# Running the experts in units of 256 tokens between the edge groups of a graph layer

## The chip, the cores and the metric

The kernel runs on one core of a Trainium2 chip. The metric is the device time of one execution in microseconds (us), as the median of several executions. In the profile PE is TensorE (the matmul engine), PEld its weight loads, DVE is VectorE, ACT is ScalarE, POOL is GpSimd, and SP is SyncE, which here only issues DMAs.

## What is computed

12500 rows of 256 numbers go through a graph layer with 212500 weighted edges and a mixing layer, and then through 8 experts. Each row goes to the one expert with the highest gate value, and each expert takes at most 1954 rows.

```python
xn = layernorm(x)
neighbor = segment_sum(edge_val[:, None] * xn[edge_src], edge_dst)
gnn = leaky(xn @ W1.T + b1 + (neighbor + neighbor * xn) @ W2.T + b2)
x = x + gnn / norm(gnn) + mix(xn)
h = layernorm(x)
idx, prb = argmax and max of softmax(h @ gate_w + gate_b)
hmid = relu(buf @ w1[e] + b1[e])          # buf: the rows of expert e, 1024 hidden
ybuf = hmid @ w2[e] + b2[e]
x = x + nan_to_num(ybuf of the row * prb * kept)
```

## The kernel before

**Stages.** A row tile is 128 rows, so there are 98 tiles. First all rows are normalised and stored to the scratch tensor `xn_d`. Then comes the edge stage, 208 pairs of edge groups. A group is 512 edges sorted by target, whose targets lie in a window of 48 rows. For each pair POOL issues eight indirect gathers of 128 rows of 256 numbers each (L552, in a ring of 24 slots, so three pairs fit); PE multiplies them with selection matrices (`multiply_pair`, L629, 16 matmul records); ACT copies the sums out of PSUM (`copy_pair`, L1348); PE transposes them (`turn_pair`, L638); DVE adds the windows to the accumulator `acc` (`add_group`, L1010), which holds all 12500 rows. A gather of pair p waits for `pair_mm` of pair p-3, that is until PE has used the rows that lie in its slots.

**The order.** It is written out at build time: `side[p]` lists what each engine does beside pair p. Pairs 0 to 55 carry the key and value products (`kv`), pairs 56 to 58 fold the weights, and from pair 59 on "C ticks" finish one row tile after another in nine steps, each step one tick after the last: the matmuls of the mixing and graph layers (L699, L709 to L716), norms on DVE and ACT, the transposes (L724), the gate logits (L734), the stores of the tile to `h2_d` and to `out`. A tile can start when all edge groups that touch it are added, so there is about 0.8 of a tile for each pair until pair 137 and then about 0.48. Routing (argmax, position in the expert's list, a table of rows by expert) runs along with it. What is left after pair 207 is done on its own.

**The experts.** They begin when the table is complete. Their order is by expert, with 4 units of up to 512 rows each, 32 units and 15632 rows in all, since the unused places of each expert are computed as well. SP loads the weights of an expert once (2 MB, L491, L492). POOL splits them into a rounded part and a rest (L565, L568), ACT and DVE split the activations in the same way, and PE computes each product in three passes of a fast 4-byte form (L785, L786, L787). Results are scaled, cleaned of NaN on DVE (L1253 to L1274), and POOL adds them to `out` by indirect DMA (L590), 128 rows at a time. POOL gathers the inputs (L579), 128 rows at a time.

## Time and profile before

| | us |
|---|---|
| median of 3 runs | 3409.26 (3408.21 to 3422.88) |
| profiled execution | 3381.42 |
| its span | 3379.7 |
| edge stage, from its first gather to its last | 106 to 2531 |
| rest of the tiles and of the routing | 2531 to 2613 |
| experts on PE | 2613 to 3359 |
| last of DVE and POOL | 3359 to 3380 |

| engine | busy us | share |
|---|---|---|
| PE | 2372.2 | 70% |
| DVE | 1748.7 | 52% |
| ACT | 1065.7 | 32% |
| POOL | 2087.9 | 62% |

How to read it: shares are means over stages that differ. PE is busy nearly all the time in the expert stage and about two thirds in the edge stage; POOL is the fuller one there. An idle time in the trace names the one that ended it; "issue" means that nothing that the profile shows was waited for, and "remote" that the releaser isn't shown. The granted clock of PE (PEclk) is given for each stretch, 1.00 being 2.4 GHz and 0.50 being 1.2 GHz.

### The profile page before, as it was taken

How to read it: one execution, taken by the hardware profiler on the slowest of the kernel's cores; microseconds unless marked ns; L12 is line 12 of the kernel's file. 1: busy time of each engine (PE TensorE's matmuls, PEld its weight loads, DVE VectorE, ACT ScalarE, POOL GpSimd, SP SyncE). 2: the span in 40 equal slices, each digit the busy share in tenths (PEclk: the TensorE clock that was granted, in tenths of full speed). 3: DMA queues.
4: the chain of work that ended last, by engine and by line, in shares of the span. 5: the costliest groups of instructions: out<-in, count | busy, mean ns of one | idle time of the engine just before them, and what ended most of it. 6: DMA issues, size and time to landing. Idle time of an engine off the chain costs nothing.

```text
span 3379.7 us, 40594 instructions
## 1 busy us (share of the span) xinstructions
PE 2372.2 (70%) x12708; PEld 1702.0 (50%) x12708; DVE 1748.7 (52%) x4466; ACT 1065.7 (32%) x2265; POOL 2087.9 (62%) x1981
## 2 busy tenths in 40 slices
PE   0277777675666757666666766656665999999997
PEld 0033333332344545454544434333344899999997
DVE  7256565553235545454544333333347577777765
ACT  5212211120123333333322212121122555555553
POOL 0466666666666666666666666666662466666663
PEclk9889888987687787787887666676776999999998
DMA  9544444443344444444444434444342221323330
GB/s 293 155 130 135 132 134 133 128 133 107 114 131 138 135 135 134 134 139 132 139 131 124 120 116 121 115 118 120 115 118 92 50 49 50 72 67 68 73 42 7
DMA packets 270446, 386.95 MB, mean 114 GB/s; under 512 B 51560, under 2 KB 210030, under 8 KB 270128
## 3 DMA queue, kind: packets, MB, share of 16 engines
q0 software_dynamic: 105984, 245.21, 27.9%
q1 hardware_dynamic: 123362, 100.70, 9.7%
q10 hardware_dynamic: 40886, 38.41, 3.4%
q8 instruction: 106, 1.74, 0.2%
q14 instruction: 108, 0.88, 0.1%
HBM read 321.97 MB, written 67.21 MB: 115 GB/s over the span
## 4 chain that ended last, share of the span: by engine, by line
PE 34%; another core or an unknown queue 17%; POOL 15%; issue 14%; DVE 12%; ACT 3%; DVEq 2%; DMA 2%; ACTq 0%; SPq 0%; POOLq 0%
POOL rows_sb L552 15%; PE bank L785 7%; PE bank L786 7%; PE bank L787 7%; PE bank L659 4%; PE bank L629 3%; DVEq L1008 2%; DVE arena L1025 1%; DVE s_sb L999 1%; DVE acc L1010 1%; PE bank L795 1%; DVE arena L1090 1%; PE bank L657 1%; PE bank L638 1%
## 5 line engine op out<-in xcount | busy, mean ns | idle before, releaser
L552 POOL DMA_INDIRECT rows_sb<-xn_scratch,src_sb x1664 | 1625.2, 977 | 902.1 <-issue 570.1
L629 PE MATMUL bank<-rows_sb,s_sb 128*48 128x256 f32 x3328 | 588.9, 445 | 263.7 <-issue 201.1
L629 PEld LDWEIGHTS bank<-rows_sb,s_sb 128*48 128x48 f32 x3328 | 248.1, 139 | 544.2 <-issue 414.6
L1010 DVE TENSOR_TENSOR acc<-acc,bank 128x96 f32 x416 | 106.1, 255 | 705.8 <-remote 398.9
L590 POOL DMA_INDIRECT out_dram<-rows_sb,sca_i x128 | 208.1, 1625 | 273.3 <-DVE rows_sb L1274 236.6
L1376 ACT ACT_TABLE_LOAD x95 | 121.9, 1283 | 618.5 <-remote 543.3
L1228 DVE TENSOR_TENSOR hid<-relu,hid 128x512 fp32r<-128x512 f32 (+1 forms) x256 | 198.3, 775 | 215.1 <-ACT relu L1443 198.0
L785 PE MATMUL bank<-w_lo,hid 128*128 128x256 f32 (+1 forms) x1024 | 298.2, 291 | 0.0
L787 PE MATMUL bank<-w_hi,hid 128*128 128x256 f32 (+1 forms) x1024 | 288.7, 282 | 0.0
L786 PE MATMUL bank<-w_hi,hid 128*128 128x256 f32 (+1 forms) x1024 | 288.7, 282 | 0.0
L1348 ACT COPY sums<-bank 112x256 f32<-112x256 f32 x208 | 77.0, 372 | 653.0 <-remote 514.6
L1441 ACT ACTIVATE hid<-bank,fb 128x512 fp32r<-128x512 f32 (+1 forms) x256 | 171.2, 669 | 337.9 <-issue 320.4
L638 PE MATMUL bank<-ident,sums 112*128 112x112 f32 x416 | 99.5, 316 | 233.1 <-DVE acc L1010 129.9
L659 PE MATMUL bank<-arena 128*128 128x512 f32 x392 | 222.2, 697 | 0.0
L638 PEld LDWEIGHTS bank<-ident,sums 112*128 112x128 f32 x416 | 48.8, 158 | 328.9 <-issue 261.0
L785 PE MATMUL bank<-xg_hl,w_hi 128*128 128x512 f32 (+1 forms) x512 | 198.6, 388 | 5.2 <-ACT relu L1443 2.6
L786 PE MATMUL bank<-xg_hl,w_hi 128*128 128x512 f32 (+1 forms) x512 | 196.4, 384 | 0.0
L787 PE MATMUL bank<-xg_hl,w_lo 128*128 128x512 f32 (+1 forms) x512 | 195.4, 382 | 0.0
L786 PEld LDWEIGHTS bank<-w_hi,hid 128*128 128x128 f32 (+1 forms) x1024 | 190.0, 186 | 4.3
L785 PEld LDWEIGHTS bank<-w_lo,hid 128*128 128x128 f32 (+1 forms) x1024 | 189.5, 185 | 4.4
L787 PEld LDWEIGHTS bank<-w_hi,hid 128*128 128x128 f32 (+1 forms) x1024 | 189.3, 185 | 0.5
L579 POOL DMA_INDIRECT rows_sb<-h_scratch,gat_i x128 | 140.0, 1093 | 65.0 <-issue 31.7
(186 smaller groups left out, 4620.9 us busy)
## 6 DMA issues: line engine op xcount, KB each, us to landing
rows_sb<-xn_scratch,src_sb POOLq DMA_INDIRECT x1664
arena<-xn_scratch SPq DMA_DIRECT2D x194, 128.0 KB
w_raw<-ffn_w_in SPq DMA_DIRECT2D x16, 1024.0 KB
xnt_scratch<-arena SPq DMA_DIRECT2D x97, 128.0 KB
arena<-xnt_scratch SPq DMA_DIRECT2D x97, 128.0 KB
arena<-x_in SPq DMA_DIRECT2D x97, 128.0 KB
h_scratch<-arena ACTq DMA_DIRECT2D x97, 128.0 KB
out_dram<-arena ACTq DMA_DIRECT2D x97, 128.0 KB
```

The costliest lines, as they stand in the source:

```text
L552: pool.indirect_dma_start(out=rows_sb[:, c % ROW_SLOTS, :], out_offset=None, in_=xn_d, in_offset=bass.IndirectOffsetOnAxis(ap=src_sb[:, c: ...
L579: pool.indirect_dma_start(out=xs_slots[s][0:r, :], out_offset=None, in_=h2_d, in_offset=bass.IndirectOffsetOnAxis(ap=gat_i[0:r, col:col + ...
L590: pool.indirect_dma_start(out=out, out_offset=bass.IndirectOffsetOnAxis(ap=sca_i[0:r, col:col + 1], axis=0), in_=yo[0:r, q % YS, i, :], in ...
L629: m = pe.matmul(psum[p % 2][i * HALF:i * HALF + WIN, 0:D], s_sb[:, p % S_SLOTS, i * GROUP + j, :], rows_sb[:, c % ROW_SLOTS, :], start=j = ...
L638: m = pe.transpose(psum[7][:, h * P:h * P + HALF + WIN], sums[:, p % SUM_SLOTS, h * P:(h + 1) * P], ident[0:HALF + WIN, 0:HALF + WIN])
L659: m = pe.matmul(kv[0:r, :], xnt[:, t % R1, h, 0:r], wkv_sb[:, h, :], start=False, stop=h == H - 1)
L785: pe.matmul(out_, s_hi.bitcast(F32R), m_lo.bitcast(F32R), start=start, stop=False)
L786: pe.matmul(out_, s_hi.bitcast(F32R), m_hi.bitcast(F32R), start=False, stop=False)
L787: return pe.matmul(out_, s_lo.bitcast(F32R), m_hi.bitcast(F32R), start=False, stop=stop)
L1010: dve.tensor_tensor(win, win, psum[7][:, 0:H * P].rearrange("p (h w) -> p h w", h=H)[:, :, g % 2 * HALF:g % 2 * HALF + WIN], ALU.add).then ...
L1228: dve.tensor_tensor(hid_lo.bitcast(F32R), relu[:, c % RELU_SLOTS, 0:n], hid_hi, ALU.subtract).then_inc(l1_rest, 1)
L1441: act.activation(hid[:, 0, f * GE * P:f * GE * P + n].bitcast(F32R), l1_bank(c)[:, 0:n], ACT.Relu, bias=fb1[:, x_, f:f + 1]).then_inc(l1_r ...
```

## The change

The experts no longer wait for the routing to end. As rows are routed, an expert that has 256 new rows puts a unit of 256 rows in a queue, and the units run in the order of the queue. There are 56 units, 14336 rows in all.

- `side` now has 326 places. Place p below 208 carries pair p. C steps of tile t stand at place `enters[t]` + step, with nearly the tiles of before for each pair. A unit has five ticks: in tick 0 PE transposes its 256 rows (L891), in ticks 1 to 4 it does the first layer for two of the eight hidden blocks each (L901), and one tick later the second layer for the same two blocks (L920). Ticks are handed out by a budget of 10.0 for a place and 2.7 for a tick, at most two to a place in the edge stage and one after it. As built, 40 ticks lie in places 101 to 137, 115 in places 138 to 207, 25 in places 208 to 220 and 101 with work of PE after them, from place 221 on. The units in places below 208 are the first 31.
- A second tick of a place does the first layer of its own blocks and then the second layer of the blocks that the first tick began, whose relus ACT must have made in between. C steps 1 and 3 stand between the two ticks.
- The products are plain 4-byte matmuls, two records each, on operands that are not split: the passes, POOL's split and the rest parts on ACT and DVE are gone.
- Each unit loads its own weights, 2.1 MB, by the expert's number, which SP reads from `expert_i`. So there are 56 loads in place of 8, from two places or more ahead, into two sets of buffers.
- POOL issues a unit's two gathers (L691) between the two groups of a pair and its two scatters (L701) behind them.
- `acc` is a lap of 32 tiles that is used again; behind it lie the experts' buffers. A tile's columns are zeroed by a DMA of 128 KB once they were read.
- `multiply_pair` has one PSUM bank in place of two and waits for the copy of the pair before. The tile products (`mix`, `gnn`) have one bank in place of two.

```diff
+LAP_TILES = 32
+UNIT_TILES = 2
...
+        w1_sb = [behind(0, H, FF) for _ in range(2)]
+        w2_sb = [behind(0, FC, D) for _ in range(2)]
+        b1_sb = [behind(0, FC) for _ in range(2)]
+        b2_sb = [behind(1, D) for _ in range(2)]
...
+            enters.append(max([FIRST_C + t * 5 // 4, ready] + [e + 1 for e in enters[-1:]]))
...
+            return max(0, ((routes[b][-1] + 1) * P - NE * (UNIT - 1)) // UNIT)
...
+        PE_PLACE, PE_EXPERT = 10.0, 2.7
+        PE_STEP = {1: 1.2, 3: 3.0, 7: 0.5, 8: 0.7}
+        e_ticks = [(k, j) for k in range(K) for j in range(TICKS)] + [(K, j) for j in range(TICKS)]
+        e_place, time, p = [], 0.0, FIRST_C
+        for k, j in e_ticks:
+            if j == 0 and k < K:
+                b = batch_of[k]
+                wanted = slots_at[b] + (4 if slots_at[b] + 4 < PAIRS else 2)
+            while True:
+                if p > last_c:
+                    if e_place and e_place[-1] == p:
+                        p += 1
+                        continue
+                    if j == 0 and k < K and p < wanted:
+                        p += 1
+                        continue
+                    break
+                if (j or k == K or p >= wanted) and time >= PE_EXPERT and e_place.count(p) < 2:
+                    time -= PE_EXPERT
+                    break
+                p += 1
+                time = min(time, PE_PLACE / 2)
+                time += PE_PLACE - (2.9 if p < PAIRS else 0.0)
+                time -= sum(v for s_, v in PE_STEP.items() if p - s_ in enters)
+            e_place.append(p)
...
+            w1_at[max([known] + [place_of(k - 1, 0)] * (k > 1))].append(k)
+            w2_at[max([known] + [place_of(k - 1, 2)] * (k > 1))].append(k)
+            lag = 3 if known < PAIRS else 1
+            gather_at[max([known - 1 + lag] + [place_of(k - 2, 0) + lag] * (k > 1))].append(k)
+            lag = 3 if place_of(k + 1, TICKS - 1) < PAIRS - 3 else 1
+            scatter_at[min(place_of(k + 1, TICKS - 1) + lag, PLACES - 1)].append(k)
...
+                sp.dma_start(acc[:, :, lap_column(t):lap_column(t) + P],
+                             far_d[:, :, bass.ds(ZERO_AT - flag * (ZERO_AT - k * P), P)]
+                             ).then_inc(acc_ld[k % len(acc_ld)], 16)
...
+            def expert_of(k):
+                sp.wait_ge(q_ready, sum(units_after(b) > units_after(b - 1) for b in range(batch_of[k] + 1)))
+                return sp.value_load(expert_i[:, UNIT_TILES * k:UNIT_TILES * k + 1], min_val=0, max_val=NE - 1)
+
+            def load_first(k):
+                x_ = expert_of(k)
+                if k >= 2:
+                    sp.wait_ge(l1_relu, relu_value(k - 2, TICKS - 1))
+                sp.dma_start(w1_sb[k % 2], ffn_w1[bass.ds(x_, 1)].rearrange("a (h p) f -> p (a h) f", p=P)
+                             ).then_inc(w1_ld[k % 2], 16)
+                sp.dma_start(b1_sb[k % 2], ffn_b1[:, bass.ds(x_, 1), :].rearrange("p a c -> p (a c)")
+                             ).then_inc(w1_ld[k % 2], 16)
+
+            def load_second(k):
+                x_ = expert_of(k)
+                if k >= 2:
+                    sp.wait_ge(y_biased, k - 1)
+                sp.dma_start(w2_sb[k % 2], ffn_w2[bass.ds(x_, 1)].rearrange("a (c p) d -> p (a c) d", p=P)
+                             ).then_inc(w2_ld[k % 2], 16)
+                sp.dma_start(b2_sb[k % 2], ffn_b2[bass.ds(x_, 1), :].broadcast_to([P, D])).then_inc(w2_ld[k % 2], 16)
...
-            sp.wait_ge(c_mm, T)
-            load_expert(0)
-            sp.dma_start(fb1[:, :, :], ffn_b1).then_inc(b1_ld, 16)
-            for x_ in range(1, NE):
-                load_expert(x_)
...
+                if k == 0 or batch_of[k - 1] != b:
+                    pool.wait_ge(q_ready, sum(units_after(i) > units_after(i - 1) for i in range(b + 1)))
+                    for t in range(max(0, routes[b][-1] + 1 - OS), routes[b][-1] + 1):
+                        pool.wait_ge(c_st[t % OS], 32 * (t // OS + 1))
+                if k >= 2:
+                    pool.wait_ge(x_turned, k - 1)
...
+                pool.wait_ge(y_done, k + 1)
...
+            for p in range(PLACES):
+                if p < PAIRS:
+                    gather_group(2 * p)
+                for k in gather_at[p]:
+                    gather_unit(k)
+                if p < PAIRS:
+                    gather_group(2 * p + 1)
+                for k in scatter_at[p]:
+                    scatter_unit(k)
...
-                if p >= 2:
-                    pe.wait_ge(pair_copied, p - 1)
+                if p >= 1:
+                    pe.wait_ge(pair_copied, p)
                 for j in range(GROUP):
                     for i in range(2):
                         c = (2 * p + i) * GROUP + j
-                        m = pe.matmul(psum[p % 2][i * HALF:i * HALF + WIN, 0:D], s_sb[:, p % S_SLOTS, i * GROUP + j, :],
+                        m = pe.matmul(psum[0][i * HALF:i * HALF + WIN, 0:D], s_sb[:, p % S_SLOTS, i * GROUP + j, :],
...
-                    mix, gnn = psum[3 + par][0:r, 0:D], psum[3 + par][0:r, D:2 * D]
+                    mix, gnn = psum[3][0:r, 0:D], psum[3][0:r, D:2 * D]
                     pe.wait_ge(c_gelu, H * (t + 1))
                     pe.wait_ge(c_summed, t + 1)
-                    if t >= 2:
-                        pe.wait_ge(c_leaky, t - 1)
-                        pe.wait_ge(c_based, t - 1)
+                    if t >= 1:
+                        pe.wait_ge(c_leaky, t)
+                        pe.wait_ge(c_based, t)
...
+            def unit_tick(n):
+                k, j = e_ticks[n]
+                bank = psum[x_bank[n]]
+                if k < K:
+                    if x_before[n] is not None:
+                        k0, j0 = e_ticks[x_before[n]]
+                        if j0 == 0:
+                            pe.wait_ge(x_copied, k0 + 1)
+                        else:
+                            pe.wait_ge(l1_relu, relu_value(k0, j0))
+                    if j == 0:
+                        pe.wait_ge(xs_ld[k % 2], 16 * UNIT_TILES * (k // 2 + 1))
+                        for i in range(UNIT_TILES):
+                            for h in range(H):
+                                m = pe.transpose(bank[:, (i * H + h) * P:(i * H + h + 1) * P],
+                                                 xs[:, k % 2 * UNIT_TILES + i, h * P:(h + 1) * P], ident[:, :])
+                        m.then_inc(x_turned, 1)
+                    else:
+                        if j == 1:
+                            pe.wait_ge(w1_ld[k % 2], 32 * (k // 2 + 1))
+                            pe.wait_ge(x_copied, k + 1)
+                        for i in range(2):
+                            f = 2 * (j - 1) + i
+                            for h in range(H):
+                                m = pe.matmul(bank[:, i * UNIT:(i + 1) * UNIT], w1_sb[k % 2][:, h, f * P:(f + 1) * P],
+                                              xt[:, k % 2, h, :], start=h == 0, stop=h == H - 1)
+                        m.then_inc(l1_mm, 1)
+
+                if n == 0:
+                    return
+                k, j = e_ticks[n - 1]
+                if k == K or j == 0:
+                    return
+                bank = psum[y_bank(k)]
+                pe.wait_ge(l1_relu, relu_value(k, j))
+                if j == 1:
+                    pe.wait_ge(w2_ld[k % 2], 32 * (k // 2 + 1))
+                    if y_bank_before(k) is not None:
+                        pe.wait_ge(y_biased, y_bank_before(k) + 1)
+
+                for f in (2 * j - 2, 2 * j - 1):
+                    tiles = range(UNIT_TILES)
+                    for i in tiles if f < FC - 1 else reversed(tiles):
+                        m = pe.matmul(bank[:, i * D:(i + 1) * D], hid[:, f, i * P:(i + 1) * P], w2_sb[k % 2][:, f, :],
+                                      start=f == 0 and i == 0, stop=f == FC - 1 and i == 0)
+                m.then_inc(l2_mm, 1)
...
+            def unit_tick(n):
+                k, j = e_ticks[n]
+                k -= 1
+                if k < 0:
+                    return
+                y = yo[:, k % YS * UNIT_TILES:(k % YS + 1) * UNIT_TILES, :]
+                mask = mask_sb.bitcast(I32)
+                if j == 1:
+                    product = psum[y_bank(k)][:, :].rearrange("p (i d) -> p i d", d=D)
+                    dve.wait_ge(w2_ld[k % 2], 32 * (k // 2 + 1))
+                    dve.wait_ge(l2_mm, (TICKS - 1) * (k + 1))
+                    if k >= YS:
+                        dve.wait_ge(y_st[k % YS], 16 * UNIT_TILES * (k // YS))
+                    dve.tensor_tensor(y, product, b2_sb[k % 2].unsqueeze(1).broadcast_to([P, UNIT_TILES, D]), ALU.add
+                                      ).then_inc(y_biased, 1)
+                elif j == 3:
+                    dve.wait_ge(y_scaled, UNIT_TILES * (k + 1))
+                    if k:
+                        dve.wait_ge(y_done, k)
+                    link(dve.tensor_tensor(mask, y, y, ALU.not_equal))
+                    link(dve.copy_predicated(y, mask, nil[:, :].unsqueeze(2).broadcast_to([P, UNIT_TILES, D])))
+                elif j == 4:
+                    link(dve.tensor_scalar(clip_sb, y, 10000.0, -10000.0, ALU.min, ALU.max))
+                    link(dve.tensor_scalar(mask, y, 0.0, 0.0, ALU.mult, ALU.not_equal))
+                    dve.copy_predicated(y, mask, clip_sb).then_inc(y_done, 1)
...
+            def unit_tick(n):
+                k, j = e_ticks[n]
+                bank = psum[x_bank[n]]
+                if k < K and j == 0:
+                    act.wait_ge(x_turned, k + 1)
+                    if k >= 2:
+                        act.wait_ge(l1_mm, l1_value(k - 2, TICKS - 1))
+                    act.copy(xt[:, k % 2, :, :].rearrange("p h (i n) -> p i h n", i=UNIT_TILES),
+                             bank[:, 0:UNIT_TILES * H * P].rearrange("p (i h n) -> p i h n", i=UNIT_TILES, h=H)
+                             ).then_inc(x_copied, 1)
+                elif k < K:
+                    act.wait_ge(l1_mm, l1_value(k, j))
+                    if k >= 1:
+                        act.wait_ge(l2_mm, l1_value(k - 1, j))
+                    for i in range(2):
+                        f = 2 * (j - 1) + i
+                        act.activation(hid[:, f, :], bank[:, i * UNIT:(i + 1) * UNIT], ACT.Relu,
+                                       bias=b1_sb[k % 2][:, f:f + 1]).then_inc(l1_relu, 1)
+                if j == 2 and k >= 1:
+                    k -= 1
+                    act.wait_ge(y_biased, k + 1)
+                    for i in range(UNIT_TILES):
+                        y, col = yo[:, k % YS * UNIT_TILES + i, :], k * UNIT_TILES + i
+                        act.activation(y, y, ACT.Copy, scale=sprb[:, col:col + 1]).then_inc(y_scaled, 1)
```

The order on PE near pair 188. L629 (L733 after) is `multiply_pair`, L638 (L742) `turn_pair`; L734 to L756 before and L806 to L858 after are C steps and routing. Before:

```order
L629 MATMUL bank1<-rows_sb,s_sb 48x256 x8
L638 MATMUL bank7<-ident,sums 128x112 x2
L629 MATMUL bank0<-rows_sb,s_sb 48x256 x8
L638 MATMUL bank7<-ident,sums 128x112 x2
L629 MATMUL bank1<-rows_sb,s_sb 48x256 x8
L638 MATMUL bank7<-ident,sums 128x112 x2
L734 MATMUL bank6<-gate_sb,arena 128x8 x2
L724 MATMUL bank2<-ident,arena 128x128 x2
L709 MATMUL bank3<-bias_hl,ones_r 128x256
```

And after, from pair 188 (L901 first layer, L920 second layer of a unit):

```order
L733 MATMUL bank0<-rows_sb,s_sb 48x256 x8
L742 MATMUL bank7<-ident,sums 128x112 x2
L856 MATMUL bank6<-arena,upper 128x56
L857 MATMUL bank6<-arena,ones 128x56
L858 MATMUL bank6<-arena,ones 128x8
L832 MATMUL bank2<-ident,arena 128x128 x2
L901 MATMUL bank4<-acc 128x256 x4
L920 MATMUL bank5<-acc 128x256 x4
L806 MATMUL bank2<-arena,weff 128x128 x4
L816 MATMUL bank3<-bias_hl,ones_r 128x256
```

Where pairs followed each other on PE with only their transposes between, unit ticks now stand between them, and all pairs use bank 0.

The order on POOL. Before, all 1664 edge gathers stand in a row, ahead of the first split of weights:

```order
L552 DMA rows_sb<-xn_scratch,src_sb 128x256 x1664
L565 CAST w_hi<-w_raw 128x4096
L568 TENSOR_TENSOR w_lo<-w_raw,w_hi 128x4096
L579 DMA rows_sb<-h_scratch,gat_i 128x256 x15
L579 DMA rows_sb<-h_scratch,gat_i 34x256
```

After, in the later edge stage (L675 edge gathers, L691 a unit's gathers, L701 its scatters):

```order
L691 DMA acc<-h_scratch,gat_i 128x256 x2
L675 DMA rows_sb<-xn_scratch,src_sb 128x256 x4
L701 DMA out_dram<-acc,sca_i 6272x256 x2
L675 DMA rows_sb<-xn_scratch,src_sb 128x256 x20
L691 DMA acc<-h_scratch,gat_i 128x256 x2
```

A unit's four transfers now stand in the row of edge gathers, within a place or behind it.

## Rows read from the trace of the kernel before

**Rows 1.** The page, part 1: busy time, share, instructions of each engine.

```profile
PE 2372.2 (70%) x12708; PEld 1702.0 (50%) x12708; DVE 1748.7 (52%) x4466; ACT 1065.7 (32%) x2265; POOL 2087.9 (62%) x1981
```

**Rows 2.** Stretches: start:end, us, busy us and count by engine, PEclk, DMA share, GB/s.

```profile
106.00:765.00 659.00, 445.46 (x2031) 238.79 (x2031) 367.43 (x706) 120.33 (x342) 447.99 (x450) 0.89 0.47 132
...
1289.00:1734.00 445.00, 299.10 (x1603) 219.27 (x1604) 220.44 (x758) 147.77 (x318) 295.22 (x305) 0.79 0.46 135
1734.00:2521.00 787.00, 509.85 (x2263) 303.33 (x2262) 284.55 (x954) 175.30 (x384) 526.24 (x545) 0.70 0.41 119
2521.00:2612.00 91.00, 55.51 (x248) 41.19 (x244) 68.16 (x244) 25.02 (x58) 21.16 (x12) 0.69 0.31 95
2612.00:3357.00 745.00, 736.84 (x4849) 674.42 (x4850) 506.26 (x798) 395.90 (x764) 435.62 (x291) 0.99 0.28 55
```

**Rows 3.** Timeline of POOL, 1988 to 2035: start, us, instruction, idle before and releaser.

```profile
1988.38 0.95 POOL L552 DMA_INDIRECT rows_sb<-xn_scratch,src_sb  x1 [3.90 <-remote]
1989.63 0.95 POOL L552 DMA_INDIRECT rows_sb<-xn_scratch,src_sb  x1 [0.30 <-issue]
...
2011.56 0.95 POOL L552 DMA_INDIRECT rows_sb<-xn_scratch,src_sb  x1 [3.28 <-remote]
...
2034.75 0.95 POOL L552 DMA_INDIRECT rows_sb<-xn_scratch,src_sb  x1 [3.32 <-remote]
```

**Rows 4.** Waits of POOL, 1289 to 2520: total us, times, longest.

```profile
POOL rows_sb L552 <- remote: 156.8, 60, 4.0
```

**Rows 5.** Waits of PE, 1734 to 2521: total us, times, longest.

```profile
PE bank L629 <- issue: 171.0, 163, 2.4
PE bank L638 <- issue: 44.9, 35, 3.0
PE bank L638 <- DVE acc L1010: 24.0, 14, 7.3
```

**Rows 6.** Timeline of all engines, 2003 to 2012, some rows of PE and ACT.

```profile
2004.68 0.34 PE L638 MATMUL bank<-ident,sums 112*128 112x112 f32 x1 [1.82 <-issue]
...
2006.77 1.36 PE L629 MATMUL bank<-rows_sb,s_sb 128*48 128x256 f32 x2 [1.75 <-issue]
...
2009.60 4.24 PE L629 MATMUL bank<-rows_sb,s_sb 128*48 128x256 f32 x14 [1.46 <-issue]
...
2011.60 0.37 ACT L1348 COPY sums<-bank 112x256 f32<-112x256 f32 x1
```

**Rows 7.** Timeline of PE, 1200 to 1240: matmuls at full and at half clock.

```profile
1206.65 1.04 PE L714 MATMUL bank<-w1g_sb,arena 128*128 128x256 f32 x4
1207.53 1.03 PE L716 MATMUL bank<-w2g_sb,arena 128*128 128x256 f32 x4
...
1216.32 1.91 PE L711 MATMUL bank<-w2m_sb,arena 128*128 128x256 f32 x4
```

**Rows 8.** The page, part 5: costliest groups, busy us, mean ns of one.

```profile
L590 POOL DMA_INDIRECT out_dram<-rows_sb,sca_i x128 | 208.1, 1625 | 273.3 <-DVE rows_sb L1274 236.6
...
L579 POOL DMA_INDIRECT rows_sb<-h_scratch,gat_i x128 | 140.0, 1093 | 65.0 <-issue 31.7
```

**Rows 9.** Timeline of POOL, first gathers of pairs 101 and 207.

```profile
1288.95 0.95 POOL L552 DMA_INDIRECT rows_sb<-xn_scratch,src_sb  x1 [1.97 <-PE bank L629]
...
2520.15 0.95 POOL L552 DMA_INDIRECT rows_sb<-xn_scratch,src_sb  x1 [3.12 <-remote]
```

**Rows 10.** Timeline of PE around it: multiplications of pairs 100 and 101.

```profile
1299.72 1.93 PE L629 MATMUL bank<-rows_sb,s_sb 128*48 128x256 f32 x16
...
1320.13 1.94 PE L629 MATMUL bank<-rows_sb,s_sb 128*48 128x256 f32 x16
```

**Rows 11.** The first expert's weights: issue by SP, then POOL's first use.

```profile
2562.49 0.40 SPq L491 DMA_DIRECT2D w_raw<-ffn_w_in  x1
```

```profile
2572.06 3.60 POOL L565 CAST w_hi<-w_raw 128x4096 fp32r<-128x4096 f32 x1 [41.46 <-DMA weff<-ffn_b_in]
```

**Rows 12.** Timeline at the end: the last matmul and the last scatter.

```profile
3358.72 0.28 PE L787 MATMUL bank<-w_hi,hid 128*34 128x256 f32 x1
...
3370.88 1.77 POOL L590 DMA_INDIRECT out_dram<-rows_sb,sca_i  x1 [0.30 <-issue]
```

More of the change, by code:

```diff
@@ L221, in build @@
+        sel = behind(1, P)
+        sprb = behind(1, SLOTS)
+        (col_i, col_odd, col_tile, col_from, full_at, some_at, count, full, fresh, ranked, queue_at, queue_base) = (
+            behind(1, 1) for _ in range(12))
         ld_gmin, ld_edges, ld_gbc = sem("ld_gmin"), sem("ld_edges"), sem("ld_gbc")
@@ new lines, in build, with small_steps @@
+        batch_of = [next(b for b in range(len(routes)) if k < units_after(b)) for k in range(K)]
+        def small_steps(p):
+            found = [("logit", t) for t, e in enumerate(enters) if e + 8 == p]
+            for b in range(len(routes)):
+                if chosen_at[b] + 1 == p:
+                    found.append(("sums", b))
+                if chosen_at[b] + 2 == p:
+                    found.append(("rank", b))
+            tiles = [t for t in range(T) if build_at[t] + 1 == p]
+            if tiles:
+                found.append(("table", tiles))
+            for b in range(len(routes)):
+                if slots_at[b] == p and units_after(b) > units_after(b - 1):
+                    found.append(("slots", b))
+            return found
@@ new lines, in build, with place_of @@
+        for n, (k, j) in enumerate(e_ticks):
+            here = at_place(e_place[n])
+            after = next((i for i, v in enumerate(here) if v == ("late", e_place[n])), len(here))
+            if ("unit", n - 1) in here or after == len(here):
+                here.append(("unit", n))
+            else:
+                here.insert(after, ("unit", n))
+        PLACES = len(side)
+        def place_of(k, j):
+            return e_place[k * TICKS + j]
+        w1_at, w2_at, gather_at, scatter_at = ([[] for _ in range(PLACES)] for _ in range(4))
@@ L398, in l2_bank @@
[L398 to L408 removed]
+        late_unit = next(k for k in range(K + 1) if place_of(k, 0) > last_c + 1)
+        x_bank, x_before, used = [], [], {}
```

809 lines of the change are left out of this document (358 added, 451 removed).

## The prediction

> **What bounds the kernel now.** I read the page's busy table first, then the stretches, then the timelines of POOL and PE. The busy table [rows 1] names no bound: PE has 70%, POOL 62%. The stretches do [rows 2]. From 2612 to 3357 PE is busy 736.84 of 745.00 us at clock 0.99, so the expert stage is bound by PE's instructions, 23.3 us for each of the 32 units. In the edge stage eight gathers make a pair, so the counts of POOL give the pace: 659.00 us for 450/8 pairs is 11.7 us a pair, 445.00 for 305/8 is 11.7, 787.00 for 545/8 is 11.55. I use 11.65. The reader should see that it hardly moves while PE's load and clock do. The timeline of POOL says why [rows 3]: gathers start 1.25 us apart (0.95 and a gap of 0.30), so eight take 10.05 us, and after two pairs POOL stands for about 3.3 us and waits for a multiplication (156.8 us over 106 pairs, 1.5 us each [rows 4]). POOL sets the pace, with a tax of 1.6 us from its round trip with PE.
>
> PE looks free there and is not quite. From 1734 to 2521 it is busy 509.85 us, 7.5 us for each of 68.1 pairs, at clock 0.70 [rows 2]. But it also stands 171.0 and 44.9 us on "issue" [rows 5], 3.2 us a pair, in which nothing visible is missing. The timeline shows such a spell [rows 6]: three matmuls begin in the five us from 2004.68 to 2009.60, the multiplication then goes on, and at 2011.56 POOL [rows 3] and at 2011.60 ACT [rows 6] move together. PE's results come late while POOL issues without a pause, and in a bunch when it pauses. That is the row on which the change will turn.
>
> **The change part by part.** I sum against the profiled execution (3381.42 us; its span is 3379.7). The median lies 27.8 us above it, and I add that at the end.
>
> *What goes.* The expert stage, 745 us, and with it the splits on POOL, ACT and DVE and the three passes.
>
> *What a unit costs on PE.* Its two layers are 32 matmuls of 256 columns, two records each. At full clock four such records take 0.88 us (1206.65 to 1207.53; at half clock up to 1.91, at 1216.32 [rows 7]), so 64 take 14.1 us; with the transposes of its rows 14.5 us, 2.9 us a tick. 56 units are 812 us. As PE work that is more than the 745 us of before: plain 4-byte products save nothing here, and the gain can come only from units that PE does beside the edge stage. 31 units lie there.
>
> *What a unit costs on POOL.* Two gathers at 1093 ns and two scatters at 1625 ns [rows 8], each with the gap of 0.30: 6.6 us. In places 101 to 137 that is 8 units in 37 places, 1.4 us a place, and with 11.65 POOL's floor is 13.1. In places 138 to 207 it is 23 units in 70 places, 2.2 us, and the floor is 13.8. These transfers are queued ahead of edge gathers, so they cost their whole length.
>
> *What a place costs PE.* Places 101 to 137 hold 40 ticks, 1.08 a place, 3.1 us. PE is busy 299.10 us over 38.1 pairs there, 7.85 us [rows 2]. With the issue stalls of the later stretch, 3.2 us, the sum is 14.15. Places 138 to 207 hold 115 ticks, 1.64 a place, 4.8 us at full clock: 7.5 + 3.2 + 4.8 = 15.5. Both are above POOL's floor, so I let PE set them: 37 x 14.15 + 70 x 15.5 = 524 + 1085 = 1609 us. I take full clock for the new ticks and the old busy time for the old work, since denser work should raise the clock and the crawl should not shrink.
>
> *Before place 101* nothing but the bank of the multiplication and the lap changes. PE reaches pair 101 at about 1311: its first gather is issued at 1288.95 [rows 9], and PE multiplies pairs 100 and 101 at 1299.72 and 1320.13 [rows 10], mean 1310. With one bank, a multiplication waits for ACT's copy of the pair before. The copy takes 0.37 us [rows 6] and has the rest of an 11.65 us pair to hide in; without that cover (both at once behind a late result) it costs 0 to 0.4 us for each of 101 pairs, 0 to 40 us. I take 0. The zeroing DMAs of the lap are 66 of 128 KB on SP, beside 130 GB/s: nothing. DVE drops to 284.55 busy of 787.00 in the later stretch [rows 2]; its finish of a unit is at most half of the 15.8 us (506.26/32) that it spends on a unit of twice the rows with its splits. Nothing.
>
> *Places 208 to 220.* 25 ticks are 72 us; the last tiles and the routing take PE 55.51 busy in 91.00 us now [rows 2], and about half of that work is still ahead. I take 100 us; the bounds are 91 and 163 (all of both).
>
> *The tail.* 101 ticks from place 221 on at 2.9 us are 293 us, at the clock of the expert stage. Then the last unit's finish and two scatters: from the last matmul at 3358.72 to 3379.7 it is 21 us now, for more tiles than a unit has [rows 12]; I take 17.
>
> *The weights.* 2.1 MB for a unit every 14.5 us in the tail. The first expert's 2.1 MB were issued at 2562.49 and used at 2572.06 [rows 11], 9.6 us. They hide behind PE with 4.9 us to spare. Each is loaded 56 times instead of 8.
>
> Sum: 1311 + 1609 + 100 + 293 + 17 = 3330 us, against 3381.42: a gain of 51. With 27.8 the median is 3358, or 1.5% below 3409.26. X, the mean of a place from 101 to 207, is 15.0 in this sum; with all else kept, no change is X = 15.5, or 16.2 in the later 70 places.
>
> *One rule beside this.* The granted clock is 0.70 to 0.79 where PE is busy 65 to 67% of a stretch, and 0.99 where it is busy 99% [rows 2]. The Trainium skill, "TensorE: Matmul & The Clock Gate", Part 1, states that the half clock is the state after idleness and that activity releases the full one; the trace agrees. If this goes all the way, the first rival below is its result. A second rule speaks against the change. The weights of a unit move beside the gathers, and the DMA share is 0.46 at 135 GB/s already [rows 2]. If a load of 9.6 us delays the pair that meets it by half of that, a third of the pairs lose 4.8 us each, 171 us in all unless the three pairs of slots hide it. The Trainium skill, "DMA: Bandwidth & Descriptors", Queues, rings and completion order, says that each DMA engine takes turns between the queues that have work, packet by packet; no row here shows two heavy queues in the edge stage. The sum leaves it at nothing, because PE takes a pair some 21 us after its first gather was issued [rows 9, 10] and the gathers themselves need only 10.
>
> **The rivals.**
>
> *POOL sets the pace (faster).* With PE at full clock its old work of 7.5 us at 0.70 would shrink to 5.3 at the least, and 5.3 + 3.2 + 4.8 = 13.3 is under POOL's 13.8. Then 37 x 13.1 + 70 x 13.8 = 1451, in all 3172, median 3200. For it speaks that the pace held at 11.7 where the load and the clock of PE differed [rows 2]. Against it speaks that POOL's pauses, in which PE's results come out, are shorter the fuller POOL is.
>
> *The ticks stand in PE's way one after another (slower).* In places 138 to 207 the second layer of one tick needs relus that ACT makes from the tick just ahead on PE. ACT sees those results late as long as POOL doesn't pause [rows 3, 6]. PE stands, the next multiplication stands behind it, POOL runs out of slots, and only then do results come out. The price is the ticks added to the pace of 11.65: 3.1/0.79 = 4.0 in the earlier places and 4.8/0.70 = 6.8 in the later, so 37 x 15.6 + 70 x 18.4 = 1865, in all 3586, median 3614. It decides from 16.2 us a place in the later stretch, 0.7 above my value.
>
> *The weights (slower).* By the sum above 171 us more: 3501, median 3529. The same in the tail: if a unit's weights took 20 us there, 20 units would add 110.
>
> *The units don't run where they should.* If the queue were ready too late and all 56 ran after the edge stage: 2521 + 91 + 812 + 17 = 3441, median 3469. The order is fixed when the kernel is built, so a late queue would hold the edge stage instead; little speaks for it.
>
> **How the numbers follow.** My forecast (X from 14.3 to 15.35) has 0.36, POOL's pace (X under 14.3) 0.17, no change within 0.5% 0.09. The ticks in series have 0.30, the weights 0.05, a late queue 0.03. A measurement of this kernel can tell about 0.5% from no change. That gives faster 0.53, same 0.09, slower 0.38. Likeliest is 3358. Its own range is 3280 to 3391. For 8 in 10 I leave out the lower end of POOL's pace and the upper end of the serial case: 3200 to 3600.
>
> **What will show it.** In the changed profile: gathers of pair 207 beginning at about 2883 (1289 + 1609 less one place of 15) against 2520 now [rows 9]; the idle time of POOL's gathers behind the multiplication, about 1.6 us a place if POOL paces and over 3 if PE does; the granted clock from 1734 on, above 0.8 in my forecast and 0.70 in the serial case; waits of the second layer (L920) for ACT's relus in the edge stage, small in mine and over 2 us a place in the serial case; 14.5 us a unit in the tail, with no wait for the weights. The prediction is wrong if places before 101 are slower than 11.65 us, if a gather beside a load lands late, or if a unit takes other than 14.5 us of PE.

## The result and the profile after

The changed kernel takes 3247.72 us in the median (3244.98 to 3249.60, 4 runs) against 3410.56 for the kernel before: ratio 0.9515, interval 0.9491 to 0.9539. It is 4.9% faster. The prediction had 3358 us, a gain of 1.5%: the sign is right, and the forecast gain is a third of the measured one. The profiled execution took 3249.6 us, 132 less than that of before, where the sum had 51.

The stretches of the changed kernel, in the columns of [rows 2]. They begin at the first gathers of pairs 101 and 138 and end with that of pair 207; the last one lies in the tail.

```profile
1311.00:1807.00 496.00, 400.09 (x2111) 310.31 (x2112) 254.62 (x846) 176.45 (x388) 323.93 (x324) 0.86 0.57 167
1807.00:2800.00 993.00, 783.05 (x3878) 577.39 (x3876) 408.74 (x1242) 286.61 (x646) 653.38 (x641) 0.87 0.54 159
...
2900.00:3200.00 300.00, 296.76 (x1420) 260.82 (x1419) 90.11 (x191) 98.01 (x226) 105.94 (x82) 0.99 0.64 178
```

496 us for 37 places is 13.4 us each and 993 for 69 is 14.4, where the prediction had 14.15 and 15.5. The granted clock rose to 0.86 and 0.87, from 0.79 and 0.70. Pairs 59 to 101 took 12.14 us each, 0.5 more than before, with no unit beside them.

What POOL and PE wait for from 1807 to 2800 in the changed kernel (us in total, times, longest), against [rows 4, 5]:

```profile
POOL rows_sb L675 <- remote: 74.6, 41, 2.3
POOL rows_sb L675 <- PE bank L733: 63.3, 13, 11.7
POOL acc L691 <- PE bank L891: 18.1, 6, 5.9
```

```profile
PE bank L920 <- ACT acc L1552: 51.5, 12, 16.8
PE bank L806 <- issue: 35.5, 14, 10.5
PE bank L742 <- DVE acc L1125: 30.6, 12, 6.4
PE bank L733 <- issue: 15.4, 27, 1.0
```

The issue stalls ahead of the multiplication fell from 2.5 us a pair (171.0 in 68) to 0.2 (15.4 in 69). PE's idle time as a whole fell much less: from 4.0 us a place (798 less 518.9 busy, in 69) to 3.0 (993 less 783.05). Of these 3.0 us, 1.7 are still "issue", now spread over many lines.

PE's busy time from 1807 to 2800 by line: second layer, first layer, transposes of the units, and the multiplication (x is the count of records, then busy us and mean ns of one; the last part is idle time ahead). Below it the multiplication of before, from 1722 to 2520:

```profile
L920 PE MATMUL bank<-acc 128*128 128x256 f32 x720 | 208.8, 435 | 64.7 <-ACT acc L1552 51.5 <-issue 12.6
L901 PE MATMUL bank<-acc 128*128 128x256 f32 x720 | 194.4, 413 | 12.5 <-issue 10.9 <-ACT acc L1543 1.3
L891 PE MATMUL bank<-ident,acc 128*128 128x128 f32 x88 | 16.4, 299 | 4.8 <-issue 4.7
L733 PE MATMUL bank<-rows_sb,s_sb 128*48 128x256 f32 x1104 | 159.6, 409 | 16.5 <-issue 15.4
```

```profile
L629 PE MATMUL bank<-rows_sb,s_sb 128*48 128x256 f32 x1112 | 272.5, 496 | 183.9 <-issue 171.0 <-DMA rows_sb<-xn_scratch,src_sb 5.4 <-DVE acc L1010 2.4
```

The units' ticks take 419.6 us, 6.1 a place, and the old work the other 5.3, where it took 7.5 before.

POOL still pauses, 156 us or 2.3 a place, against 1.6 before. Its timeline near the last pair shows a unit's gathers (L691) among the edge gathers, and pauses of the old kind [rows 3]:

```profile
2777.99 0.95 POOL L691 DMA_INDIRECT acc<-h_scratch,gat_i  x1 [0.30 <-issue]
...
2787.80 0.95 POOL L675 DMA_INDIRECT rows_sb<-xn_scratch,src_sb  x1 [2.34 <-remote]
...
2799.78 0.95 POOL L675 DMA_INDIRECT rows_sb<-xn_scratch,src_sb  x1 [2.25 <-PE bank L733]
```

The tail on PE: one unit from its transposes (L891) to those of the next, and the end.

```profile
2944.09 0.60 PE L891 MATMUL bank<-ident,acc 128*128 128x128 f32 x4
...
2958.35 0.60 PE L891 MATMUL bank<-ident,acc 128*128 128x128 f32 x4
...
3227.42 3.62 PE L920 MATMUL bank<-acc 128*128 128x256 f32 x16
```

14.26 us a unit, back to back, and 17 us from the end of the last matmul (3231) to 3247.9.

### The profile page after: what moved, and what is told of

Same layout as the page of the kernel before. It is cut to its first block, busy times and chain, and to the rows that moved or that the text cites. A ratio compares the mean times of both kernels' runs of the same rounds, so it can differ in the third digit from the quotient of the medians.

```text
span 3247.9 us, 39751 instructions
## 1 busy us (share of the span) xinstructions
PE 2389.5 (74%) x11820; PEld 1735.3 (53%) x11820; DVE 1506.5 (46%) x4274; ACT 922.1 (28%) x2112; POOL 1932.7 (60%) x1905
## 4 chain that ended last, share of the span: by engine, by line
PE 36%; another core or an unknown queue 25%; issue 16%; DVE 11%; ACT 7%; DVEq 2%; DMA 1%; ACTq 1%; POOL 1%; SPq 0%; POOLq 0%
PE bank L920 9%; PE bank L901 8%; PE bank L733 5%; PE bank L763 3%; PE bank L806 2%; PE bank L818 1%; DVEq L1123 1%; PE bank L823 1%; PE bank L821 1%; DVE arena L1140 1%; ACT L1509 1%; PE bank L742 1%; PE bank L867 1%; ACT acc L1552 1%
## 5 line engine op out<-in xcount | busy, mean ns | idle before, releaser
L675 POOL DMA_INDIRECT rows_sb<-xn_scratch,src_sb x1664 | 1640.6, 986 | 953.1 <-issue 559.3
L733 PE MATMUL bank<-rows_sb,s_sb 128*48 128x256 f32 x3328 | 461.9, 410 | 100.5 <-issue 42.9
L920 PE MATMUL bank<-acc 128*128 128x256 f32 x1792 | 471.6, 408 | 68.4 <-ACT acc L1552 51.5
L901 PE MATMUL bank<-acc 128*128 128x256 f32 x1792 | 456.6, 400 | 14.6 <-issue 12.2
L920 PEld LDWEIGHTS bank<-acc 128*128 128x128 f32 x1792 | 361.1, 205 | 136.7 <-ACT acc L1552 59.1
L901 PEld LDWEIGHTS bank<-acc 128*128 128x128 f32 x1792 | 352.9, 202 | 72.9 <-issue 25.0
L733 PEld LDWEIGHTS bank<-rows_sb,s_sb 128*48 128x48 f32 x3328 | 218.9, 131 | 303.6 <-issue 171.3
L701 POOL DMA_INDIRECT out_dram<-acc,sca_i x112 | 180.3, 1610 | 264.7 <-DVE acc L1348 238.8
L1552 ACT ACTIVATE acc<-bank,acc 128x256 f32<-128x256 f32 x448 | 187.7, 471 | 504.9 <-PE bank L901 253.7
L806 PE MATMUL bank<-arena,weff 128*128 128x128 f32 (+1 forms) x784 | 143.1, 338 | 148.6 <-issue 111.6
L806 PEld LDWEIGHTS bank<-arena,weff 128*128 128x128 f32 x784 | 130.0, 244 | 166.7 <-issue 164.1
L742 PE MATMUL bank<-ident,sums 112*128 112x112 f32 x416 | 88.4, 294 | 147.8 <-DVE acc L1125 110.1
L761 PE MATMUL bank<-bkv_hl,ones_r 128*128 128x512 f32 x98 | 52.2, 532 | 172.7 <-DVE arena L1140 111.0
L742 PEld LDWEIGHTS bank<-ident,sums 112*128 112x128 f32 x416 | 44.1, 146 | 242.7 <-issue 231.9
L691 POOL DMA_INDIRECT acc<-h_scratch,gat_i x112 | 109.4, 977 | 88.9 <-PE bank L891 56.1
L1493 ACT ACTIVATE arena<-bank 128x512 f32<-128x512 f32 x98 | 58.7, 599 | 297.6 <-PE bank L763 142.9
```

Of the source, the lines that this page charges most:

```text
L675: pool.indirect_dma_start(out=rows_sb[:, c % ROW_SLOTS, :], out_offset=None, in_=xn_d, in_offset=bass.IndirectOffsetOnAxis(ap=src_sb[:, c: ...
L691: pool.indirect_dma_start(out=xs[:, k % 2 * UNIT_TILES + i, :], out_offset=None, in_=h2_d[0:tokens, :], in_offset=bass.IndirectOffsetOnAxi ...
L701: pool.indirect_dma_start(out=out[0:tokens, :], out_offset=bass.IndirectOffsetOnAxis(ap=sca_i[:, col:col + 1], axis=0), in_=yo[:, k % YS * ...
L733: m = pe.matmul(psum[0][i * HALF:i * HALF + WIN, 0:D], s_sb[:, p % S_SLOTS, i * GROUP + j, :], rows_sb[:, c % ROW_SLOTS, :], start=j == 0, ...
L742: m = pe.transpose(psum[7][:, h * P:h * P + HALF + WIN], sums[:, p % SUM_SLOTS, h * P:(h + 1) * P], ident[0:HALF + WIN, 0:HALF + WIN])
L806: m = pe.matmul(psum[2][:, f * P:f * P + r], weff[:, h, f * P:(f + 1) * P], c_xnt[:, t % XS, h, 0:r], start=h == 0, stop=h == H - 1)
```

## The experiments

Two theories. **Stalls add**: PE's busy time, its issue stalls and the new ticks make up a place (the prediction's step). **POOL prices a unit**: POOL's queue and its round trip with PE set the pace, a unit in the edge stage costs its 6.6 us of POOL, and PE's stalls give way to work.

The runs fell on several chips, and this must be known to read them: on two of them the kernel before took 3095 and 3099 us, on the others 3374 to 3411. I call these the quick and the late chips; why, the last section tells. Times are compared with the kernel before, or the changed one, measured on the same chip, unless it is said otherwise. Only the late chips also ran the changed kernel itself: ratio 0.9515 in the result, 0.9534 (r_after) and 0.9561 (u_after, 0.9546 to 0.9577), so its gain there is 4.4 to 4.9%. All paces are from first gather to first gather of pairs 138 and 207, unless said.

**The overlap as a whole.** All units behind the last tile step, the same instructions:

```diff
-                wanted = slots_at[b] + (4 if slots_at[b] + 4 < PAIRS else 2)
+                wanted = last_c + 2
```

> The changed kernel with every unit put behind the last tile step, so that all 56 run after the edge stage with the same instructions. The overlap is the gain: on a core as in the result the edge stage goes back to about 11.8 us a place, then 91 us and 56 x 14.25 = 798 us, in all 3440 to 3480, slower than the kernel before by 1 to 2%. On the faster core 3100 to 3170, at the kernel before or up to 2% over it. If the three-pass form rather than the place of the units was the cost: clearly under the kernel before.

Measured 3515.3 us (one execution), where on the same chip the changed kernel took 3247.3 and the kernel before 3407.6. That is above the expected range.

> The changed kernel itself, unaltered, as the reference for the kernels beside it. The kernel before took 3099 us in the runs of the first experiments, where a pair took 10.2 us and POOL never waited, against 3410 in the result, where a pair took 11.65 us with 1.6 us of waiting. If POOL's queue sets the pace: on such a core 10.2 + 1.4 and 10.2 + 2.1 us a place, 2860 to 2890 us, ratio to the kernel before 0.92 to 0.935; on a core as in the result 3245 to 3260, ratio 0.95. If PE's work sets it: 2950 to 3000 on the faster core.

The first gather of pair 207 in r_late and in r_after:

```profile
2593.69 0.95 POOL L675 DMA_INDIRECT rows_sb<-xn_scratch,src_sb  x1 [0.30 <-issue]
```

```profile
2791.93 0.95 POOL L675 DMA_INDIRECT rows_sb<-xn_scratch,src_sb  x1 [2.28 <-remote]
```

So without the overlap the change is 3.2% slower. Its edge stage ended at 2594 against 2792 with the units in it and 2520 before: 31 units cost the edge stage 198 us, 6.4 us each, and each saves 14.26 in the tail. 6.4 us is what POOL's four transfers take in the changed kernel (977 ns a gather, 1610 a scatter, and the gaps), and less than half of what the ticks take on PE. That the size fits does not yet show the cause; the next runs part the two. And the change without any unit in them made the places longer: 12.2 us from 59 to 101, 12.3 to 138, 12.0 later, against 11.65, 11.7 and 11.6.

**POOL's share and PE's share.** First the units' transfers left out on POOL in the edge stage (waits kept, results of those units left out; the scatters likewise by `moved_out`), then the matmuls of units 4 to 29 over 8 of 256 columns in both layers:

```diff
+        def moved_in(k):
+            return k < 2 or not any(k in gather_at[p] for p in range(PAIRS))
...
                 if k >= 2:
                     pool.wait_ge(x_turned, k - 1)
+                if not moved_in(k):
+                    return
```

```diff
+            def columns(k):
+                return 8 if 4 <= k < 30 else D
...
+                                m = pe.matmul(bank[:, i * UNIT:i * UNIT + columns(k)],
+                                              w1_sb[k % 2][:, h, f * P:(f + 1) * P], xt[:, k % 2, h, 0:columns(k)], start=h == 0, stop=h == H - 1)
```

> Without the units' transfers on POOL in the edge stage. Where the kernel before takes 3410 us: POOL's queue and its waits set the pace, 12.0 to 12.6 us in places 138 to 207 against 14.3, about 3060 to 3100 us in all; PE sets it: over 14 us and over 3200 us. Where it takes 3095: 2690 as before.

> The matmuls of units 4 to 29 over 8 columns. Where the kernel before takes 3410 us: POOL's queue sets the pace, 14.0 to 14.5 us in places 138 to 207, 3220 to 3260 us; PE sets it: 11.5 to 12.8 us, 3080 to 3130 us. Where it takes 3095: 2860 as before.

> The changed kernel itself, as the reference for the two beside it. On a core where the kernel before takes 3410 us: 3245 to 3260. On one where it takes 3095: POOL's queue alone, 10.3 + 1.4 and 10.3 + 2.1 us a place and some 0.3 for PE, 2860 to 2900 us, ratio 0.93; if PE's 11.35 us of busy time and its waits matter there, up to 2950.

On a late chip (kernel before 3374.4, changed 3224.4): without transfers 3088.3 us, pace 12.95 against 14.31; with 8 columns 3222.4 us, pace 14.20. So POOL's transfers are worth 1.4 of their 2.1 us a place, where a pace set by PE alone would hardly have moved. The stretches of the changed kernel (u_after), of the one without transfers and of the one with 8 columns (the columns of [rows 2]; places 138 to 207):

```profile
1783.00:2770.00 987.00, 775.53 (x3878) 573.32 (x3877) 407.06 (x1241) 286.02 (x644) 650.85 (x640) 0.87 0.55 160
```

```profile
1746.00:2640.00 894.00, 727.39 (x3890) 553.14 (x3888) 408.26 (x1243) 286.31 (x646) 538.28 (x553) 0.91 0.53 164
```

```profile
1786.00:2766.00 980.00, 736.43 (x3876) 568.14 (x3874) 406.42 (x1242) 286.65 (x642) 650.83 (x641) 0.70 0.55 162
```

The third has the clock at 0.70 where the changed kernel has 0.87. Second layer, first layer and multiplication in it, from 1785 to 2765:

```profile
L923 PE MATMUL bank<-acc 128*128 128x8 f32 x720 | 128.2, 304 | 57.5 <-ACT acc L1555 33.1 <-issue 24.0
L904 PE MATMUL bank<-acc 128*128 128x8 f32 x720 | 110.4, 278 | 24.4 <-issue 22.2 <-ACT acc L1546 1.9
L733 PE MATMUL bank<-rows_sb,s_sb 128*48 128x256 f32 x1104 | 213.9, 518 | 29.2 <-issue 27.9
```

Its ticks take 3.7 us a place instead of 5.9, and the other work 7.0 instead of 5.3: most of the time that the columns took away came back at the slower clock. PE's busy time fell by only 0.6 us a place, from 11.2 to 10.7, and the pace by 0.1. This run is therefore a weak test of PE's share on a late chip, weaker than its expectation took it to be.

Without transfers the pace came out above the expected 12.0 to 12.6. PE is busy 10.5 of 12.95 us, and POOL's pauses grew from 2.3 to 3.0 us a place (206 us in all). With no unit at all a place took 12.0 (r_late, another late chip). So of the 2.3 to 2.4 us that the units add to a place in this stretch, the ticks alone account for about 0.9 and the transfers for 1.4; in places 101 to 137 it is 0.1 (12.38 against 12.30) and 0.8 (13.22 less 12.38). POOL's queue has the larger part, and PE is not free.

The same kernels on the two quick chips:

> The changed kernel without the units' gathers and scatters that POOL issues in the edge stage (except the first two gathers; those units compute on old rows and their results are left out); the waits before them stay. POOL has 6.6 us less for each unit, 2.1 us a place later and 1.4 earlier. POOL sets the pace: 14.4 falls to about 12.3 and 13.4 to 12.0, the kernel 170 to 220 us faster than the changed one. PE sets it: the pace stays above 14 and 13.2, the kernel within 30 us.

> The changed kernel, with the matmuls of units 4 to 29 over 8 columns instead of 256: all instructions, waits and transfers stay, PE's array time for them goes (about 2 us of 2.9 a tick, 3.3 us a place in the later stretch); the result of these columns is left out. PE sets the pace: 14.4 us a place falls to 11.5 to 12.5 in places 138 to 207, the kernel is 150 to 250 us faster than the changed one. POOL sets it: 13.8 to 14.4 stays, the kernel within 40 us of the changed one.

They took 2686.1 and 2857.2 us, and again 2690.4 (s_nodma) and 2859.6 (s_cols8), with the kernel before at 3099.1 and 3094.9. The pace is 10.3 without transfers (full columns) and 12.26 with them (8 columns), and POOL hardly pauses in either, so the whole 2.0 us of POOL's transfers shows there. The changed kernel itself never fell on a quick chip; its gain there stays open.

**Do PE's stalls add?** The kernel before, with each pair's 16 records issued three times:

```diff
-                for j in range(GROUP):
+                for j in [*range(GROUP)] * 3:
```

> The kernel before with the multiplication of each pair issued three times over (3.9 us of PE more for a pair), wanted where the kernel before takes 3370 to 3410 us. Stalls stay and add to PE's work, as the prediction had it: 14.6 us a pair in the later edge stage, 250 to 450 us slower. Stalls are idle time that gives way to work: 11.6 to 12.4 us a pair there, 0 to 100 us slower, with the issue idle ahead of the multiplication under 1 us a pair.

On a late chip 3642.8 us against 3396.8, ratio 1.072 (1.070 to 1.074): 246 us slower, just under the 250 to 450 expected if stalls add, while its pace lies nearer to the other theory. The pace went from 11.6 to 12.7 us and by 1.5 and 1.7 in the two stretches ahead of it. Of 3.9 us more on PE a pair, 1.2 to 1.7 came through. The clock rose to 0.88, so in the later stretch PE's busy time rose from 7.5 to 9.9 us a pair and its idle time fell from 4.0 to 2.9. What PE waited for from 1900 to 2700:

```profile
PE bank L699 <- ACT arena L1400: 85.6, 20, 4.8
PE bank L629 <- issue: 51.4, 78, 1.7
PE bank L699 <- issue: 36.4, 6, 9.2
```

The stall ahead of the multiplication fell from 2.5 to 0.8 us a pair. So neither theory holds whole: the stalls there mostly give way, but a part of PE's work does reach the pace. On the quick chips (b_triple and s_triple, with a like expectation) the same kernel took 3172.1 and 3169.3 us against 3099.1 and 3094.9. From pair 59 on it took 10.2 us a pair, as the kernel before with one bank does (s_onebank; the kernel before itself has no profile there). The 73 to 74 us more lie in pairs 0 to 56 (655 us against 583 in s_onebank), where key and value products fill PE.

> The kernel before, with only two of the four gathers of every edge group issued from the seventh group on (the others' rows are left out, PE multiplies what lies in the slots). POOL needs 5.0 us a pair instead of 10.05. Stalls stay: PE needs 7.5 busy and 3.2 stalled, so the later edge stage runs at about 10.7 us a pair. Stalls come from POOL's gathers and go with them: 7 to 8.5 us a pair there, with under 0.7 us of issue idle of the multiplication a pair. In the stretch with 0.8 tiles a pair PE's work of 7.2 to 8 us bounds it in both.

With half of the edge gathers left out (quick chip, 2460.0 us) a pair took 6.7, 7.6 and 5.8 us in the three stretches from 59 on (the last under both expectations). That is about what PE and the rest need on such a chip where POOL's gathers do not bind.

**How many units pay?** A budget of 11.5 for a place, so that 34 units run below place 208, closer together:

```diff
-        PE_PLACE, PE_EXPERT = 10.0, 2.7
+        PE_PLACE, PE_EXPERT = 11.5, 2.7
```

> The changed kernel with a budget of 11.5 instead of 10.0 for a place: ticks stand closer, 34 units instead of 31 in places below 208. POOL's queue decides: each unit moved from the tail costs 6.6 us there and saves 14.25, so about 23 us faster than the changed kernel, 0.7%. If PE's work decides in the denser places (places with two ticks in a row): no gain or up to 40 us slower.

3262.2 us, ratio to the kernel before 0.9595 (0.9577 to 0.9612), against 0.9515, 0.9534 and 0.9561 for the changed kernel, which was not measured on this chip: slower by 0.4 to 0.8%, where 0.7% faster was expected from POOL's queue. Places 101 to 137 now hold 1.5 ticks and took 14.5 us, 1.1 to 1.2 more than with 1.08 ticks, 2.5 to 2.9 us for each tick added. POOL's transfers are 1.3 of that. The rest is longer pauses of POOL, 2.8 us a place instead of 2.3, while PE is busy 12.0 us of the place instead of 10.8. Together that is near PE's price of a tick (2.9 in the tail), and then a unit costs about what it saves. Where a place has less tile work, from 138 on, 1.64 ticks still cost 1.5 us each (14.39 less 12.0 of r_late). So the turn lies near one tick a place beside 0.8 of a tile, and above 1.6 beside half a tile.

**The weights.** Loads only for the first two units:

> The changed kernel with weights loaded only for the first two units; the other 54 loads of 2.1 MB are left out, and those units compute with the weights that lie there. If the loads hide, as the prediction has it: within 0.5% of the changed kernel, tail units still 14.2 us. If they delay gathers beside them: up to 170 us faster, with the pace of places 138 to 207 lower by 1 us or more and POOL's wait for the multiplication smaller.

3256.8 us (one execution) against 3247.3 (3241.7 to 3253.6): no gain. 54 loads of 2.1 MB beside the gathers cost nothing that shows, and the pace (14.5) did not fall. The delay by loads that the prediction weighed does not come here.

**The 0.5 us of places 59 to 101.** One bank for the multiplication in the kernel before, and in the changed kernel steps 3 and 1 in the other order on PE:

```diff
-                if p >= 2:
-                    pe.wait_ge(pair_copied, p - 1)
+                if p >= 1:
+                    pe.wait_ge(pair_copied, p)
```

```diff
-                    for t, s in c_steps(k, (1, 3)):
+                    for t, s in c_steps(k, (3, 1)):
```

> The kernel before with all pairs multiplied into one PSUM bank, as in the change. On the core without late results it cost nothing. Where the kernel before takes 3370 to 3410 us: if it is what makes places from 59 on longer (12.1 to 12.2 us against 11.65, with or without units), 12.0 to 12.3 us a pair from 59 on and 50 to 90 us slower than the kernel before; if the cause is another part, within 15 us.

> The changed kernel with steps 3 and 1 of the tile work on PE in this order instead of 1 and 3, so that ACT's copy of the turned tile has the products of step 3 to hide behind before step 1 needs it. If PE's stall before step 1 (61.2 us of issue and 12.2 us of waiting for ACT in 42 places, against 13.6 and 4.4 before the change) is what made places 59 to 101 0.5 us longer, it is worth up to 0.5 us a place over 149 places, 20 to 75 us faster than the changed kernel on a core as in the result. If POOL sets the pace without waiting, nothing: within 0.3%.

One bank: 3408.9 us, ratio 1.0037 (1.0024 to 1.0050), 11.75 us from 59 to 101 and 11.84 from 138 on, against 11.64 and 11.57 in the profile of before, which is of another chip; on the quick chip nothing (s_onebank, 3096.3 against 3094.9). The order: 3244.9 against 3247.3, places 59 to 101 at 12.06 instead of 12.2 and 101 to 138 at 13.5 instead of 13.4. So the bank is at most 0.1 us of the 0.5 there. PE's stall before step 1 shrank from 59.1 us of issue to 20.7, and other stalls grew (issue ahead of the multiplication from 8.0 to 29.6). The bank of the tile products and the lap were not tried alone; what makes the rest stays open. Of the kernels that leave nothing out, none beat the changed kernel beyond its interval.

## Why the prediction was wrong

The sum, term by term, against the profile after:

| term | forecast us | measured us |
|---|---|---|
| to PE's start of pair 101 | 1311 | 1333 (1311 + 22) |
| places 101 to 137 | 524 | 496 |
| places 138 to 207 | 1085 | 1007 (70 x 14.39) |
| 208 to the end | 410 (100 + 293 + 17) | 412 (108 + 287 + 17) |
| profile to median | +28 | -2 |

- **Right**: plain products save nothing on PE; 14.5 us a unit (14.26); the last tiles, the tail with its 101 ticks and the drain (410 against 412); the weights hide; the gain comes from overlap alone (r_late).
- **The step that failed** is "Both are above POOL's floor, so I let PE set them", that is 7.5 + 3.2 + 4.8 = 15.5 us a place from 138 on. PE's time does not set the pace by adding up: with POOL's transfers left out and all ticks kept, a place took 12.95 us instead of 14.31 (u_nodma), and 3.9 us more of PE's work a pair brought 1.2 to 1.7 (v_triple). Both stretches came out near the floor of 13.1 and 13.8 that the prediction had worked out for POOL, at 13.4 and 14.4. The 0.3 and 0.6 us above it are of the size of what the change adds to a place without units (0.6 and 0.4, r_late).
- **The terms of that step.** The three terms are 5.3 + 3.0 + 6.1 in the changed kernel. The old work was not fixed at 7.5: the granted clock went from 0.70 to 0.87, its busy time fell to 5.3, which is the figure of the faster rival, and the multiplication alone fell from 272.5 us to 159.6. The ticks took 3.7 us of PE each beside the gathers, not the 2.9 of the tail. The 3.2 us were read off two lines, and on these two "issue" fell to 0.3; but all idle time of PE together was 3.0, so a term of that size was not wrong as a size, only as a fixed need. Two errors, of -2.2 and +1.3, partly cancel: that the forecast is no further off is luck in part.
- **The clock.** The Trainium skill, "TensorE: Matmul & The Clock Gate", Part 1, says that the throttled clock is the default and that activity releases it. The trace agrees in direction: the granted clock was 0.70 before and 0.87 after, and 0.70 again with 8 columns (u_cols8).
- **The rival that came.** POOL's pace, with a chance of 0.17, was the mechanism in the main. Its 1451 us for places 101 to 207 stand against 1503 measured, 14.05 a place. By the prediction's own sign, POOL's pauses would be 1.6 us a place if POOL paces and over 3 if PE does. They were 2.3: between the two, as the 0.9 us of the ticks in u_nodma are.
- **Too small by 22 us**: the stretch before place 101, put at no change. The bounds of 0 to 40 us held it, the value of 0 did not, and the one bank for which they stood accounts for little of it (v_onebank).
- **The serial rival** (0.30) did not come. Second layers waited for ACT's relus 51.5 us in 69 places, 0.7 us each, where it wanted over 2.
- **The step to the median.** The profiled execution of before took 3381.42 us and is none of the timed ones (3408 to 3423), so it lay 28 us below their median; the one of after lay 2 us above. An offset of one kernel was carried to the other; that is 30 of the 110 us missed. The kernel before had medians from 3374 to 3411 on the late chips, so the 28 us are no larger than the difference from one chip to another; whether that is their cause no run shows.

## What to carry to other kernels

The idle time of an engine, and its busy time at a low clock, are not fixed costs to which new work adds: here 7.5 us of old work became 5.3 when ticks stood beside it. First ask which queue the new work must pass that sets the pace, here the indirect transfers of POOL at 1.3 to 1.9 us each. Price a moved unit by what it puts in that queue (6.4 us in, 14.3 us out), and stop where a second engine fills; how many ticks a place bears depends on what else stands in it. And when the profiled execution of a kernel differs from its median, do not carry the difference to another kernel as a term.

## What the runs showed of the hardware

The same kernel took 9 to 10% longer on one kind of chip than on the other, and the engines' own speeds do not explain it: an edge gather takes 0.95 us with a gap of 0.30 on both, and from the first gather of pair 207 to the end the kernel with one bank takes 858 us on the quick chip and 857 on the late one. The waits of the edge stage do. The kernel before with one bank, places 138 to 207, first on a quick chip (3096.3 us), then on a late one (3408.9 us), what POOL and then PE waited for the longest:

```profile
POOL rows_sb L552 <- issue: 168.6, 553, 0.3
```

```profile
PE bank L629 <- DMA rows_sb<-xn_scratch,src_sb: 297.0, 62, 8.5
```

```profile
POOL rows_sb L552 <- issue: 156.5, 512, 0.4
POOL rows_sb L552 <- PE bank L629: 68.0, 20, 10.2
POOL rows_sb L552 <- remote: 56.4, 20, 3.4
```

```profile
PE bank L629 <- issue: 154.9, 123, 7.7
PE bank L629 <- ACT sums L1348: 67.6, 16, 9.7
```

On the quick chip POOL never pauses and PE waits for rows, as the program is written. On the late one PE's instructions begin late with nothing visible missing, and POOL waits for PE. This is 1.6 us a pair there, 229 us from pair 59 to pair 207, and 78 us more lie in pairs 0 to 56. The stalls are absent in the expert stage of both, where PE is busy 99% of the time and POOL issues few gathers. That the stream of gathers holds up PE's signals on those chips fits this, but no run tried it alone. Each chip on record was used in one set of runs only, so whether the difference belongs to the chip, and what it is, stays open. A margin tuned on one of them (how far POOL runs ahead, how many ticks stand in a place) need not hold on the other.
